# A graph network on one core: grouped dense weights, aggregate steps between one-hots, bias in the first term

## What is computed

```python
# part 1: three graph convolutions
dinv = rsqrt(segment_sum(1, dst))
h_list = [x]
for l in range(3):
    hw  = h_list[l] @ conv_w[l].T
    agg = segment_sum(hw[src] * (dinv[src] * dinv[dst])[:, None], dst)
    h_list.append(elu(agg + conv_b[l]) + h_list[l])
y  = concatenate(h_list, axis=1) @ lin_w.T + lin_b
x1 = layernorm(x + y)                      # over the 128 features
# part 2: relational convolution, 8 relations made of 4 bases
W   = einsum('rb,bio->rio', w_comp, bases)
agg = segment_sum(x1[src] * edge_weight[:, None], edge_type * N + dst)   # (8, N, 128)
out = layernorm(x1 + einsum('rni,rio->no', agg, W))
```

## Time and profile before

| | us |
|---|---|
| median of 3 runs | 1109.1 (1108.5 to 1109.4) |
| the profiled execution | 1110.0 |
| its span | 1108.2 |
| layer 0, its aggregates and one-hots | about 49 to 285 |
| layers 1 and 2, the rest of part 1 | 285 to 541 |
| part 2, 14 chunks | 541 to 1108 |

### The profile page before, as it was taken

How to read it: one execution, slowest core, us unless ns; L and a number is a source line. 1 busy time by engine, 2 the same in 40 slices (tenths; PEclk the granted TensorE clock), 3 DMA queues, 4 the chain that set the end, 5 groups by cost and what they waited for, 6 DMA issues and landing times.

```text
span 1108.2 us, 23482 instructions
## 1 busy us (share of the span) xinstructions
PE 1013.3 (91%) x9508; PEld 665.9 (60%) x9508; DVE 802.2 (72%) x1702; ACT 444.9 (40%) x1027; POOL 510.5 (46%) x542
## 2 busy tenths in 40 slices
PE   1677898889999999999399999999999999999997
PEld 1565565556644475448266666666666666666664
DVE  4689999898526764898786677777677777767753
ACT  1588898888400030004443233233233333333320
POOL 5044000000047700000377777777777777777773
PEclk9877999899999999999589999999999999999999
DMA  5263000000101010010522222222222222222221
GB/s 155 57 193 87 7 1 2 1 1 1 59 15 27 18 59 1 1 58 14 134 54 54 59 54 58 60 54 58 59 54 58 59 53 58 59 51 58 58 53 36
DMA packets 48801, 55.34 MB, mean 50 GB/s; under 512 B 15543, under 2 KB 39129, under 8 KB 48182
## 3 DMA queue, kind: packets, MB, share of 16 engines
q0 software_dynamic: 16240, 31.95, 11.5%
q1 hardware_dynamic: 32454, 21.87, 6.9%
HBM read 42.10 MB, written 8.49 MB: 46 GB/s over the span
## 4 chain that ended last, share of the span: by engine, by line
PE 68%; DVE 18%; issue 6%; SPq 2%; ACT 2%; DMA 2%; DVEq 1%; POOL 0%
PE ps L1684 21%; PE ps L1537 21%; PE ps L1663 11%; PE ps L1678 9%; DVE arena L1107 8%; SPq L681 2%; PE ps L1526 2%; DVE dinv_all L1336 2%; DVE hT L1296 1%; PE ps L1697 1%; PE ps L1691 1%; DVE u L1330 1%; PE ps L1484 1%; DMA dinv_col<-dinv_scratch 1%; DVE arena L1259 1%
## 5 line engine op out<-in xcount | busy, mean ns | idle before, releaser
L837 POOL DMA_INDIRECT arena<-x_scratch,arena x437 | 413.4, 946 | 164.6 <-issue 126.2
L1537 PE MATMUL ps<-arena,u 125*128 125x480 fp8e5 (+1 forms) x1575 | 361.3, 356 | 1.2 <-ACT arena L891 1.2
L972 ACT COPY arena<-ps 125x400 f32<-125x400 f32 x364 | 170.2, 525 | 354.6 <-PE ps L1678 325.6
L1684 PE MATMUL ps<-arena,u 125*128 125x448 f32 x650 | 297.8, 539 | 0.0
L1537 PEld LDWEIGHTS ps<-arena,u 125*128 125x128 bf16 x1575 | 153.1, 98 | 108.1 <-ACT arena L891 1.7
L1663 PE MATMUL ps<-hT,arena 128*128 128x160 f32 x874 | 200.0, 321 | 2.6 <-DVE hT L1296 2.1
L1107 DVE TENSOR_TENSOR arena<-arena 128x2048 bf16<-128x2048 bf16 (+2 forms) x158 | 188.7, 1253 | 16.5 <-PE ps L1526 13.4
L1663 PEld LDWEIGHTS ps<-hT,arena 128*128 128x128 f32 x874 | 144.1, 190 | 87.3 <-issue 74.1
L1526 PE MATMUL ps<-arena 128*128 128x125 bf16 x1256 | 150.5, 234 | 32.4 <-DVE arena L1107 30.7
L1678 PEld LDWEIGHTS ps<-dinv_all,u 64*128 64x128 bf16 x4368 | 109.1, 96 | 103.5 <-issue 82.8
L1526 PEld LDWEIGHTS ps<-arena 128*128 128x128 bf16 x1256 | 108.2, 105 | 86.0 <-DVE arena L1107 47.9
(11 more groups left out here) (187 smaller groups left out, 712.9 us busy)
## 6 DMA issues: line engine op xcount, KB each, us to landing
arena<-x_scratch,arena POOLq DMA_INDIRECT x437
arena<-hT SPq DMA_DIRECT2D x2, 1562.5 KB, 7.1
edge_scratch<-arena SPq DMA_DIRECT2D x5, 403.0 KB, 5.2
arena<-in_x_dram SPq DMA_DIRECT2D x1, 1562.5 KB
dinv_all<-dinv_scratch SPq DMA_DIRECT2D x1, 1562.5 KB, 8.3
h_scratch<-hT SPq DMA_DIRECT2D x1, 1562.5 KB, 6.1
first_term_scratch<-arena SPq DMA_DIRECT2D x1, 1562.5 KB
arena<-first_term_scratch SPq DMA_DIRECT2D x1, 1562.5 KB
```

The lines of the kernel that those rows point to most:

```text
L837: nc.gpsimd.indirect_dma_start(out=gat[:, j, :], out_offset=None, in_=x1_d, in_offset=bass.IndirectOffsetOnAxis(ap=idxg[:, j:j + 1], axis= ...
L972: nc.scalar.copy(o, ps[0:BLK, octet_bank(k, w), 0:4 * ND].rearrange("p (i m) -> p m i", i=4)).then_inc(s_se, 1)
L1537: return T.matmul(ps[:, agg_bank(l, c), 0:CW[c]], u[0:BLK, s, k, :], region[:, s, 0:CW[c]], start=(first and s == 0 and k == 0), stop=(end ...
L1684: last = T.matmul(ps[:, 5, 0:NB * DN].rearrange("p (b n) -> p b n", b=NB), xb[0:BLK, s, :], sD[half][0:BLK].rearrange("p (b v) n -> p b v ...
```

## The change

1. *Layer 0.* DVE's loop over one-hot pairs is written out, and `post(0, c-2)` is cut into four steps, one behind each of the pairs 2 to 5 of the chunk. ACT's exponential goes behind the third pair of groups. The waits and the two operations on `wposf` move along.
2. *Bias.* lin_b is loaded as one row (SP) and a row of ones is set (POOL). In the first term each block gets a second matmul, ones (K = 1) times the row, into the same bank. The addition on DVE and the replicated load are gone.
3. *Part 2.* PE does octets two at a time in four banks: (2, 3) and (6, 7). The accumulator of the first batches is narrower (HB 7 to 4), the finishes go to bank 0's upper 128 columns and to bank 5, `finish_dense(c-1)` goes from tile 18 to tile 10, `finish(c-1)` from tile 24 to 15, and dense matmuls of the new half wait for the statistics of the one before. DVE's order follows: `stats_dense` at q = 6, `ahead_of(c, 4)` at q = 7, `stats` and `lower` at q = 8.
4. *The end.* The last half's dense matmuls go two to a tile, its finish one tile sooner; the fold of the five last nodes has its own buffer and comes ahead of the statistics.

The core of the diff:

```diff
@@ -55,10 +55,10 @@
-    KR = QA - (-23 * QD // TPB)
+    KR = QA - (-16 * QD // TPB)
@@ -90,8 +90,9 @@
-    SPLIT = (P * BT) * 7 // TPB - WBACK
-    HB = 7
+    SPLIT = (P * BT) * 4 // TPB - WBACK
+    LW = P * (4 * BT - 1) // TPB + WN
+    HB = 4
@@ -265,11 +275,11 @@
-        OCTET_BANKS = ((6, 7), (2, 6), (7, 2))
+        OCTET_BANKS = ((2, 3), (6, 7))
...
-            return (6, 2)[w] if k % QD == QD - 1 else OCTET_BANKS[k % QD % 3][w]
+            return OCTET_BANKS[k % 2][w]
@@ -684,6 +695,8 @@
+            sp.wait_ge(s_idxs, 1)
+            sp.dma_start(linrow[0:1, :], lin_b.rearrange("(o d) -> o d", o=1)).then_inc(s_row, 16)
@@ -780,6 +792,7 @@
             pool.wait_ge(s_idxs, 1)
+            nc.gpsimd.memset(onesrow[0:1, :], 1.0).then_inc(s_one, 1)
@@ -922,11 +935,11 @@
                     write_block(c, 0, slot)
-                if c >= 2:
-                    exps(0, c - 2)
...
                         write_block(c, i, slot)
+                    if c >= 2 and i == 2:
+                        exps(0, c - 2)
@@ -1136,22 +1149,26 @@
-            def post(l, c):
+            def post(l, c, steps=range(4)):
...
                 b = convb[:, ds(l, 1)]
+                if 0 in steps:
+                    dve.wait_ge(s_agg, NCH * l + c + 1)
...
+                if 1 in steps:
...
+                if 2 in steps:
...
+                if 3 in steps:
+                    dve.wait_ge(s_exp, NCH * l + c + 1)
@@ -1197,21 +1214,18 @@
             for c in range(1, NCH):
-                for pair in range(2):
-                    onehots(GPC * c + 2 * pair, pair, False)
-                if c == 2:
-                    dve.wait_ge(s_u, NUB)
...
-                if c >= 2:
-                    post(0, c - 2)
-                if c == 4:
...
-                with dve.Fori(1, (GPC if c < NCH - 1 else LASTG) // SLOTS) as i:
-                    for pair in range(2):
-                        onehots(i * SLOTS + (GPC * c + 2 * pair), pair, False)
+                for t in range((GPC if c < NCH - 1 else LASTG) // 2):
+                    onehots(GPC * c + 2 * t, t % 2, False)
+                    if c == 2 and t == 1:
+                        dve.wait_ge(s_u, NUB)
...
+                    if c >= 2 and 2 <= t < 6:
+                        post(0, c - 2, (t - 2,))
+                    if c == 4 and t == 7:
@@ -1244,11 +1258,10 @@
                 if c == RELS // 2 + 1:
-                    dve.wait_ge(s_back[4], 16)
-                    link(V.tensor_tensor(yt[0:BLK], yt[0:BLK], linbB[0:BLK, None, :].broadcast_to([BLK, NBLK, D]), ALU.add))
...
+            dve.wait_ge(s_back[4], 16)
@@ -1354,20 +1367,20 @@
-                def stats(c, bank=3):
+                def stats(c, bank=0):
...
-                def stats_dense(h, bank=3):
+                def stats_dense(h, bank=5):
@@ -1407,23 +1420,26 @@
                             octet(c, QA)
+                            octet(c, QA + 1)
+                        if q == 6 and rank >= 1:
+                            if rank == 1:
+                                dve.wait_ge(s_x1r, 48)
+                            stats_dense(c - 1)
...
                             indices(c, 2)
-                        for k in range(QA + 1, end):
+                        if q == 7 and rank >= 1:
+                            ahead_of(c, HB)
+                        for k in range(QA + 2, end, 2):
                             if STEP.index(k - QA) - 1 in range(BT * q, BT * q + BT):
-                                prepare(c, k)
-                                octet(c, k)
-                        if q == 8 and rank >= 1:
-                            ahead_of(c, HB)
-                            if rank == 1:
-                                dve.wait_ge(s_x1r, 48)
-                            stats_dense(c - 1)
+                                for m in (k, k + 1):
+                                    prepare(c, m)
+                                    octet(c, m)
...
                             indices(c + 1, 0, following)
-                        if q == 9:
+                        if q == 8:
@@ -1449,15 +1465,14 @@
                 ahead_of(C, 2)
+                link(V.tensor_tensor(few, accN[0][:, :, AT:AT + LNODES], carry[:, :, 0:LNODES], ALU.add))
                 stats_dense(DH - 1, 6)
-                stats(C - 1)
-                norm_dense(DH - 1, False)
-                few = aggf[:, :, 0:LNODES]
-                link(V.tensor_tensor(few, accN[0][:, :, AT:AT + LNODES], carry[:, :, 0:LNODES], ALU.add))
...
                 V.tensor_tensor(few, accN[2][:, :, 0:LNODES], few, ALU.add).then_inc(s_af, 1)
+                norm_dense(DH - 1, False)
+                stats(C - 1, 3)
+                stats_last()
                 norm(C - 1, False)
-                stats_last()
@@ -1564,10 +1579,13 @@
                         pe.wait_ge(s_linI, 1)
+                        pe.wait_ge(s_row, 16)
+                        pe.wait_ge(s_one, 1)
...
                     for q, s in enumerate(blocks_of(j)):
-                        last = T.matmul(ps[0:BLK, 7, D * q:D * (q + 1)], hT[:, BLK * s:BLK * (s + 1)], linI[:, :], start=True, stop=True)
+                        last = T.matmul(ps[0:BLK, 7, D * q:D * (q + 1)], hT[:, BLK * s:BLK * (s + 1)], linI[:, :], start=True, stop=False)
+                        last = T.matmul(ps[0:BLK, 7, D * q:D * (q + 1)], onesrow[0:1, :], linrow[0:1, :], start=False, stop=True)
@@ -1667,8 +1685,8 @@
                     pe.wait_ge(s_md, 2 * (c * QD + (k + 1)))
-                    if k >= 1:
-                        pe.wait_ge(s_se, c * (2 * QD) + 2 * k - 1)
+                    if k >= 2:
+                        pe.wait_ge(s_se, c * (2 * QD) + 2 * (k - 1))
@@ -1686,15 +1704,15 @@
-                def finish(c, bank=3):
+                def finish(c, bank=0):
                     for b in range(NB):
...
-                def finish_dense(h, bank=3):
+                def finish_dense(h, bank=5):
...
                     for b in range(NB):
@@ -1717,20 +1736,20 @@
                             pe.wait_ge(s_se, c * (2 * QD) + 2 * QD)
+                            if rank >= 1:
+                                pe.wait_ge(s_dv, c)
...
                         if rank >= 1:
-                            if j == 18:
-                                if rank >= 2:
-                                    pe.wait_ge(s_fv, c - 1)
+                            if j == 10:
                                 finish_dense(c - 1)
-                            if j == 24:
+                            if j == 15:
                                 pe.wait_ge(s_af, c)
-                                pe.wait_ge(s_dv, c)
...
                         k = QA + STEP[j + 1]
-                        if STEP[j] < STEP[j + 1] < QD and k < end:
+                        if STEP[j] < STEP[j + 1] < QD and STEP[j + 1] % 2 == 0 and k < end:
                             octet(c, k)
+                            octet(c, k + 1)
@@ -1748,16 +1767,16 @@
                     tile(C, j, LTILES)
-                    if j < DLEFT:
-                        dense(TPB - DJ + j, 0)
-                    if j == LTILES - 1:
+                    for k in range(2 * j, min(2 * j + 2, DLEFT)):
+                        dense(TPB - DJ + k, 0)
+                    if j == LTILES - 2:
+                        pe.wait_ge(s_dv, DH - 1)
                         finish_dense(DH - 1, 6)
-                        pe.wait_ge(s_af, C)
-                        pe.wait_ge(s_dv, DH - 1)
-                        finish(C - 1)
+                pe.wait_ge(s_af, C)
+                finish(C - 1, 3)
...
                 for b in range(NB):
-                    last = T.matmul(ps[0:LNODES, 7, 0:D], aggf[:, b, 0:LNODES], basesS[:, b, :], start=(b == 0), stop=(b == NB - 1))
+                    last = T.matmul(ps[0:LNODES, 7, 0:D], few[:, b, :], basesS[:, b, :], start=(b == 0), stop=(b == NB - 1))
```

More of the change, by code:

```diff
@@ L57, in build_program @@
     KC = QA - (-DLEFT * QD // TPB)
-    KR = QA - (-23 * QD // TPB)
+    KR = QA - (-16 * QD // TPB)
     NP3 = 3 * NB
     ND = NB * NBLK
-    assert NCHK == DH + 1 and DN == 8 * QD and KC < QD <= KR < QA + QD - 1 and PG <= 6
+    assert NCHK == DH + 1 and DN == 8 * QD and KC < QD <= KR < QA + QD - 1 and PG <= 6 and QA % 2 == 0 and QD % 2 == 0
     PADN = 4095
@@ L214, in build_program @@
         h_old = [carve(at, N, fp32, 4) for at in (0, A_H1, A_H2)]
+        linrow = carve(0, D, fp32, 4)
+        onesrow = carve(512, BLK, fp32, 4)
         srcI = carve(12544, TS, u32, 4)
@@ L220, in build_program @@
         wE = carve(A_W, EC, fp32, 4)
-        linbB = carve(A_LB, D, fp32, 4)
         nodeD = carve(A_NODE, PAIRS, fp32, 4)
@@ L242, in build_program, with turned @@
         aggD = work[:, 2, 0:NB * DN].rearrange("p (b n) -> p b n", b=NB)
-        accN = [ps[:, k, 0:NB * P].rearrange("p (b n) -> p b n", b=NB) for k in range(3)]
+        accN = [ps[:, k, 0:NB * w].rearrange("p (b n) -> p b n", b=NB) for k, w in enumerate((LW, P, P))]
```

(27 more changed lines are left out.)

43 lines of the change are left out of this document (20 added, 23 removed).

## The result

The changed kernel takes 1112.5 us (median of 20 runs), the kernel before 1109.3 (20 runs); the ratio is 1.0033, with a 95% interval of 1.0019 to 1.0047. The forecast was 1091, the range 1083 to 1099. Among the experiments one launch of the kernel before took 4021 us, three times the others, and is left out.

The account below looks back on a forecast made before the run. The prediction took DVE to bound layer 0 and PE the relational stage; savings of 11.5 (layer 0), 2.05 (layer 2) and 4.7 (relational stage) sum to 18.2 us, from 1109.1 to 1091, range 1083 to 1099.

Parts of the forecast that it names:

- The bias's price: Layer 0, chunk 0: 25 added one-row matmuls cost 1.5 us at the end, range 0 to 8.6.
- The sentence on the Trainium skill: Layer 0's bias: load time goes by columns, not K, so one-row matmuls take PE as long as full ones, 8.6 us.
- What is late next: Relational stage: PE waits 2.5 us a chunk for DVE's ahead_of, chunks stay at 42.0; 12 chunks bring 0.5.
- the rest of the chunk, 39.5 - 16.8 = 22.7, follows: Relational stage: PE's work behind the wait for ahead_of takes 22.7 us, making the chunk 42.0.
- Layer 0's chunks: Layer 0: chunks fall to DVE's own work, 30.4 us; chunks 2 to 5 save 11.7, gross 13.0 with chunks 1 and 6.
- the loop: Layer 0: writing out DVE's one-hot loop saves 0.16 us a turn, 5 turns a chunk.
- the steps: Layer 0: aggregate operations between one-hots remove the gaps their block makes on PE, four chunks' worth of 2 to 4 us.
- Layer 2: Removing DVE's 3.49 us bias addition saves 2.05 us, since the next aggregate then waits for PE's last row.
- the first gather and chunk 0 of part 2: Relational stage's start: 2.4 us won up to tile 15, then 4 or 5 pairs at 0.3; 3.8 us saved.
- the end: Last outputs: five nodes fold sooner but the last full chunk's output bounds the queue; 0, up to 1.5 us either way.
- Rival 3: Relational stage: the wait for ahead_of is 4.0 us or more, giving back all gains, 1115 us at 4.5; chance 0.07.
- Rival 1: Relational stage: the wait ends before PE comes, POOL bounds, chunks of 41.3 to 41.5, 1083.5 us; chance 0.20.

Follow-up runs that it names:

- the full-row form: Kernel with early ahead_of, its 512-column bias matmuls replaced by 25 over all 128 rows (127 bias rows zero); 0.975 of the kernel before, 1276 us.
- experiment 6: Changed kernel plus thirty matmuls of zeros on PE ahead of its wait for ahead_of; 1.047 of the kernel before, 1372 us.
- experiment 3: Changed kernel with DVE's ahead_of two batches sooner, ahead of batch 6; 0.986 and, again, 0.983 of the kernel before, 1290 us.
- the repaired kernels: Changed kernel with ahead_of two batches sooner (0.986, 0.983), or with that plus one 512-column one-row bias matmul a step (0.975, 1278 us).

## Why the prediction was wrong

- **The bias's price, 1.5 us with a top of 8.6, was the first failure**: in the profile of the changed kernel it is 15.3 (145.8 against 130.5 without it). The step that failed is the bound: "the nearest is L1570's own, so 8.6 us is the top". It priced the added matmuls and not what they do to their neighbours. With one of each in turns, 100 records cost 0.2 us instead of 50 at 0.11; that is 15 us more of PE's work at full clock. At half clock it is 36 us (100 at 0.36) where the 50 alone would be 10.5. How much of it reaches the end is up to the clock. The same code with 25 one-row matmuls gave 145.8, 141.8, 138.0, 145.5, 134.0, 141.8 and 144.5 for the first aggregate in seven profiles: 3.5 to 15.3 over 130.5, 11 in the mean. In the run with 134.0 the granted clock was 1.00 from 64 to 98 us, over all 100 records; in the one with 145.8 it was 0.50 from 68.7 to 89.2. Why it fell in one and not in another is open.
- **The sentence on the Trainium skill** that stood there, from "TensorE: Matmul & The Clock Gate", section LDWEIGHTS, says that the load goes by columns and not rows. The traces agree: in the run with 134.0 a weight load of one row takes 180 ns in the mean and one of 128 rows 186. By it the added matmuls come to the same 8.6. The other place cited of the same page of the Trainium skill, section The mechanism, bears on what went wrong: a load overlaps running matmuls only when it goes to other rows. I used it for octets and tiles, and did not ask it of one row against 128 in turns. The 0.11 to 0.2 us of the records would fit a lost overlap, but the full-row form also loads the same rows and stays at 0.11; so what exactly is lost with one row and 128 in turns stays open.
- **"What is late next" was right**: PE waits for ahead_of, 2.2 us in the longest for a forecast of 2.5; the pair is 1.21 as forecast (0.66 + 0.55), the short chunk 42.1 for 42.0. What was left out is the clock behind it, and that is the second failure: "the rest of the chunk, 39.5 - 16.8 = 22.7, follows" has all of it at full clock. In 6 of 11 chunks 1.67 came on top: 10.0 of the 11.0 us that part 2's chunks lost. The rows ahead of the prediction had the like, windows of 0.90 and 0.95 in layer 0, where I named the low clock behind idle time and gave it no price here. That idle time ahead brings the half clock is shown by experiment 6, on its chip; on the first chip it is read from the trace, and why five of eight equal waits were followed by it and three not is open.
- **Layer 0's chunks** were right to 0.4 us in the sum of four. On the experiments' chips the loop gives 5.0, for 0.16 a turn or 4 in all in the forecast, and the steps 5.5, for 9. Chunk 1, which has no aggregate and so shows the loop alone, wins 1.4 on the first chip for a forecast of 0.8. From chunk 1's start on the first chip won 14.2, the others 10.5; there the kernel before had less half clock to lose (7 us from 130 us to the end of layer 0, for 17 on the first chip). The split between loop and steps was not measured on the first chip.
- **Layer 2** was right (2.08 for 2.05), the first gather and chunk 0 of part 2 brought 2.4 for 3.8, the end was better (-1.6 for 0).
- **The rivals.** Rival 3, the slower side, had the right place, ahead_of, and 0.07. It asked for a wait of 4 us; it needed only 2, with the clock. On the experiments' chips it came true in size, 7.7 us, 7.5 a chunk, 1.051, but for a reason that it did not have: the late release of octets. Rival 1 is what experiment 3 makes of it; how far it goes on the first chip, where POOL's 41.3 us would bind, was not measured.

Open: the repaired kernels were not timed on the first chip. By the table above they should win there what the two failures cost, but that is argued and not shown: what moving ahead_of brings on the other chips goes by their longer wait.

## What to carry to other kernels

Price a matmul of another shape by what it does in turn with its neighbours, not by itself: put the odd shape once a group, or pad it to the neighbour's rows. Price a wait of PE by its length and, on top, by a stretch of the instructions behind it at half clock (here 1.67 us behind six of eleven waits of 0.1 to 2.2), above all where it returns in each turn of a loop. And where an operation that another engine waits for stands behind work that nobody waits for yet, move it ahead: it was one line, and worth 6.5% on the slower chips.
